# Last two batches of an early-fusion block: routing products in the score banks, batch 6 routed behind batch 7's rows, the last bias addition behind the scatter

## The reference

```python
h = tok_ref(x, ...)                       # ccm, curve, 3 channels -> 1, clipped
h = concatenate([h, txt], axis=1)         # 8 x 384 x 256
h = h + attn_ref(layernorm(h), W_DKV, W_UK, W_UV, W_UQ, W_O)
# ffn_ref(layernorm(h)):
scores = softmax(xf @ router_w)           # 3072 tokens x 8 experts
expert_weights, top_experts = top_k(scores, 2)
for k in range(2):                        # capacity 384 tokens per expert and k, in order of token
    y = dispatch_compute(xf, top_experts[:, k], w1, w2, capacity)
    out = out + y * expert_weights[:, k][:, None]
h = h + out + bias
```

## Time and profile before

| | us |
|---|---|
| three timed runs | 773.05, 773.74, 775.08 |
| their median | 773.74 |
| the profiled execution, device time | 771.72 |
| its span, from the first to the last instruction | 770.0 |
| first load of the expert half starts at | 467.35 |

### The profile page before, as it was taken

One profiled execution on the slowest core, in us unless ns is written; L12 is line 12 of the kernel. 1 busy time (PEld: TensorE's weight loads), 2 busy tenths in 40 slices (PEclk: granted clock), 3 DMA queues, 4 the chain that ended last, 5 costly groups with the idle time before them and its releaser, 6 DMA issues. The chain is left out here.

```text
span 770.0 us, 13676 instructions
## 1 busy us (share of the span) xinstructions
PE 644.2 (84%) x5136; PEld 517.6 (67%) x5136; DVE 419.1 (54%) x1003; ACT 388.3 (50%) x806; POOL 306.6 (40%) x393
## 2 busy tenths in 40 slices
PE   0435789998998999989998514999999999999993
PEld 0112445666665665656675314999999999999993
DVE  5522746868687886976875433544444444444320
ACT  2332547676574856746566004555445544554540
POOL 4100000010030402104042353977888888888234
PEclk9977989999999989999999655999999999999997
DMA  5155564637364442535620123444444444542113
GB/s 184 41 133 163 146 170 119 182 97 195 88 159 107 125 113 70 133 78 135 198 78 24 52 73 105 148 97 97 97 104 103 104 97 118 133 115 42 21 21 41
DMA packets 58978, 82.90 MB, mean 108 GB/s; under 512 B 6048, under 2 KB 50218, under 8 KB 58912
## 3 DMA queue, kind: packets, MB, share of 16 engines
q1 hardware_dynamic: 46480, 66.72, 30.3%
q0 software_dynamic: 9216, 12.41, 9.7%
q10 hardware_dynamic: 3216, 2.89, 1.2%
HBM read 50.30 MB, written 31.78 MB: 107 GB/s over the span
## 5 line engine op out<-in xcount | busy, mean ns | idle before, releaser
L1386 DVE TENSOR_TENSOR hl<-h,hh 128x384 fp32r<-128x384 f32 x128 | 103.6, 809 | 156.2 <-ACT h L1343 156.0
L921 DVE TENSOR_REDUCE mx<-s_bank 128x2 f32<-128x256 f32 (+2 forms) x192 | 124.3, 685 | 75.6 <-PE s_bank L505 74.9
L1340 ACT ACTIVATE hh<-t_bank 128x384 fp32r<-128x384 f32 x128 | 63.0, 492 | 133.5 <-PE t_bank L1428 131.2
L763 ACT ACTIVATE pt<-t_bank 128x512 f32<-128x512 f32 x128 | 76.4, 597 | 75.1 <-PE t_bank L526 73.2
L1309 POOL DMA_INDIRECT out<-yo,xr x48 | 74.8, 1558 | 72.2 <-ACT yo L1351 62.4
L1299 POOL TENSOR_TENSOR wl<-wr,wh 128x256 fp32r<-128x256 f32 x112 | 94.6, 877 | 1.2
L504 PE MATMUL s_bank<-ks,qs 96*128 96x128 bf16 (+2 forms) x384 | 81.5, 280 | 12.2 <-DMA ks<-qk_scratch 11.6
L525 PE MATMUL t_bank<-qs,ks 98*128 98x384 bf16 (+2 forms) x384 | 86.8, 278 | 5.0 <-DMA qs<-mT 4.2
L1428 PE MATMUL t_bank<-xh,wh 128*128 128x384 f32 x256 | 87.0, 340 | 0.0
L1428 PE MATMUL t_bank<-xl,wh 128*128 128x384 f32 x256 | 86.6, 338 | 0.0
L1428 PE MATMUL t_bank<-xh,wl 128*128 128x384 f32 x256 | 86.4, 337 | 0.0
(11 more groups left out here) (159 smaller groups left out, 1488.2 us busy)
## 6 DMA issues: line engine op xcount, KB each, us to landing
wr<-in_L_ffn_w SPq DMA_DIRECT2D x16, 1024.0 KB, 6.0
qk_scratch<-part SPq DMA_DIRECT2D x96, 96.0 KB
slot_rows<-empty SPq DMA_DIRECT2D x6, 1040.0 KB, 10.7
xr<-slot_rows SPq DMA_DIRECT2D x16, 390.0 KB, 3.3
wr<-in_x SPq DMA_DIRECT2D x7, 768.0 KB, 13.6
qs<-qk_scratch SPq DMA_DIRECT2D x16, 288.0 KB
ks<-qk_scratch SPq DMA_DIRECT2D x16, 288.0 KB
qs<-qk_scratch SPq DMA_DIRECT2D x16, 192.0 KB
```

The lines of the kernel that those rows point to most:

```text
L763: ins = act.activation(pt[:, p, unit // 2, 0:AT[1]], bank, ACT.Exp)
L921: ins = dve.tensor_reduce(mx[:, p // 2, j, 2 * (p % 2):2 * (p % 2) + 2], pair_region(s_bank, j), AX_X, ALU.max)
L1340: act.activation(hh[:, f, :], h_banks[f % NH], ACT.Gelu_apprx_tanh)
L1386: dve.tensor_tensor(hl[:, f, :], h[f % 2][:, :], hh[:, f, :].bitcast(F32), ALU.subtract).then_inc(hl_done, 1)
```

## The change

The batches 0 to 5 are untouched. For batches 6 and 7:

- The logits of the router go to `s_bank[0]` and the rank products to `s_bank[1]` instead of to `bank1`, with a ledger key of their own, "late".
- In turn 16 `contexts_back(15, 1)` stands before `router(6)`.
- `project(7, 1)` writes `s_bank[2]` and follows `project(7, 0)` in turn 16; DVE's two `residual(7)` follow each other there too.
- `ranks(6)` stands behind both. DVE's `keep_ranks(6)` stands behind `variances2(7)`, and `weigh(6)` and `place(6)` behind `scaled2(7)`.
- The second `rows_back(7)` writes `t_bank[2]` (M[1]) instead of `bank0`.
- POOL adds the bias of batch 7 behind its loop, that is behind `send(7)`; the store of batch 7 waits for it as before.

```diff
+        OVER = 2 * B
+        def logit_bank(b):
+            return C[:, T:T + NT * E] if b < B - 2 else s_bank[:, 0, 0:NT * E]
+        def rank_bank(b):
+            return C[:, T:T + NT * KE] if b < B - 2 else s_bank[:, 1, 0:NT * KE]
+        def project_bank(b, k):
+            return s_bank[:, 2, :] if b == B - 1 and k else M[0]
+        def rows_bank(b, c):
+            return M[1] if b == B - 1 and c else M[0]
...
@@ POOL
-                    if live(b - 1):
+                    if live(b - 1) and b < B:
                         residual(b - 1)
+            residual(B - 1)
             for q in range(2):
                 pool.wait_ge(sent[q], 16 * (B // 2) * NT * TOPK)
...
@@ TensorE, helpers
-            def project(b, k, bank):
+            def project(b, k):
                 pe.wait_ge(cn_sb, 2 * b + 2)
-                take(bank, hid_add, 2 * b + k + 1)
+                take("last" if b == B - 1 and k else 0, hid_add, 2 * b + k + 1)
+                dst = project_bank(b, k)
...
-            def rows_back(b, c, bank):
+            def rows_back(b, c):
                 pe.wait_ge(row_done, (NT + 1) * b + NT)
-                take(bank, rowT_sb, KC * b + c + 1)
+                take(1 if b == B - 1 and c else 0, rowT_sb, KC * b + c + 1)
...
+            def route_key(b):
+                return "C" if b < B - 2 else "late"
...
@@ TensorE, turns
                     if p == 1:
                         routed = not odd and live(b - 2)
-                        if routed:
+                        if routed and n < OVER:
                             router(b - 2)
                         if prev:
-                            contexts_back(n - 1, 1, routed)
+                            contexts_back(n - 1, 1, routed and n < OVER)
+                        if routed and n >= OVER:
+                            router(b - 2)
...
-                        routed = not odd and live(b - 2)
+                        routed = not odd and live(b - 2) and n != OVER
...
-                        if p == 0 and live(b - 1):
-                            project(b - 1, 1, 0)
+                        if p == 0 and live(b - 1) and n < OVER:
+                            project(b - 1, 1)
...
                         if p == 3 and live(b - 1):
-                            project(b - 1, 0, 0)
+                            project(b - 1, 0)
+                        if p == 3 and n == OVER:
+                            project(b - 1, 1)
+                            ranks(b - 2)
...
@@ DVE, turns
                     if odd:
-                        if p == 0 and live(b - 2):
+                        if p == 0 and live(b - 2) and n != OVER + 1:
                             weigh(b - 2)
                             place(b - 2)
-                        if p == 0 and live(b - 1):
-                            residual(b - 1, 1, 0)
+                        if p == 0 and live(b - 1) and n < OVER:
+                            residual(b - 1, 1)
                         if p == 1 and live(b - 1):
                             norms2(b - 1)
                             variances2(b - 1)
+                        if p == 1 and n == OVER + 1:
+                            keep_ranks(b - 2)
                         if p == 2 and live(b - 1):
                             scaled2(b - 1)
+                        if p == 2 and n == OVER + 1:
+                            weigh(b - 2)
+                            place(b - 2)
...
-                        if p == 3 and live(b - 2):
+                        if p == 3 and live(b - 2) and n != OVER:
                             keep_ranks(b - 2)
...
                         if p == 3 and live(b - 1):
-                            residual(b - 1, 0, 0)
+                            residual(b - 1, 0)
+                        if p == 3 and n == OVER:
+                            residual(b - 1, 1)
```

More of the change, by code:

```diff
@@ L578, in contexts_out @@
                 mm.then_inc(cnT_ps, 1)
-            def project(b, k, bank):
+            def project(b, k):
                 pe.wait_ge(cn_sb, 2 * b + 2)
-                take(bank, hid_add, 2 * b + k + 1)
+                take("last" if b == B - 1 and k else 0, hid_add, 2 * b + k + 1)
+                dst = project_bank(b, k)
                 for at, t in enumerate((0, 1) if k == 0 else (2,)):
                     for c in range(KC):
-                        mm = pe.matmul(M[bank][:, at * DIM:(at + 1) * DIM], cn[:, c, t * P:(t + 1) * P], wo[:, c, :],
+                        mm = pe.matmul(dst[:, at * DIM:(at + 1) * DIM], cn[:, c, t * P:(t + 1) * P], wo[:, c, :],
                                        start=(c == 0), stop=(c == KC - 1))
@@ L650, in ranks @@
                 pe.wait_ge(oh_done, b + 1)
-                take("C", step, ROUTER_STEPS * b + RANK_STEP)
+                take(route_key(b), step, ROUTER_STEPS * b + RANK_STEP)
                 for t in range(NT):
-                    dst = C[:, T + t * KE:T + (t + 1) * KE]
+                    dst = rank_bank(b)[:, t * KE:(t + 1) * KE]
                     pe.matmul(dst, tri[:, :], ohb[:, t, :], start=True, stop=False)
@@ L731, in _ @@
                         if p == 3 and live(b - 1):
[L732 removed]
+                            rows_back(b - 1, 1)
                     else:
@@ L828, in token_values, with rows_back @@
                 act.activation(vb[b % 2][:, tiles, :, 0:HD], src, ACT.Copy).then_inc(v_sb, 1)
-            def rows_back(b, c, bank):
+            def rows_back(b, c):
                 act.wait_ge(rowT_ps, KC * b + c + 1)
-                act.activation(rowT[:, c, :], M[bank][:, 0:T], ACT.Copy).then_inc(rowT_sb, 1)
+                act.activation(rowT[:, c, :], rows_bank(b, c)[:, 0:T], ACT.Copy).then_inc(rowT_sb, 1)
             def gates(b):
@@ L949, in normalise, with residual @@
                 dve.tensor_tensor(dst, src, by, ALU.mult).then_inc(cxn_done, 1)
-            def residual(b, k, bank):
+            def residual(b, k):
                 dve.wait_ge(wo_ps, 2 * b + k + 1)
                 tiles = slice(0, 2) if k == 0 else slice(2, 3)
-                src = M[bank][:, 0:(2 - k) * DIM].rearrange("p (t d) -> p t d", d=DIM)
+                src = project_bank(b, k)[:, 0:(2 - k) * DIM].rearrange("p (t d) -> p t d", d=DIM)
                 dve.tensor_tensor(hid[:, b, tiles, :], hid[:, b, tiles, :], src, ALU.add).then_inc(hid_add, 1)
@@ L1046, in choose @@
                 dve.wait_ge(log_ps, b + 1)
-                then(dve.tensor_copy(logits[:, :, :], C[:, T:T + NT * E].rearrange("p (t e) -> p t e", t=NT)))
+                then(dve.tensor_copy(logits[:, :, :], logit_bank(b).rearrange("p (t e) -> p t e", t=NT)))
                 for t in range(NT):
```

16 lines of the change are left out of this document (8 added, 8 removed).

## The result

| us | before | after |
|---|---|---|
| median of six timed runs each | 772.23 | 764.69 |
| their range | 768.05 to 775.08 | 763.59 to 767.08 |
| the profiled execution | 771.72 | 767.08 |
| last context copy to first load of the expert half | 43.79 | 37.85 |
| expert half, from that load to the end | 302.6 | 302.5 |

After divided by before is 0.9904, with a 95% interval from 0.9875 to 0.9934. The changed kernel is faster, by 0.66 to 1.25%. The forecast of 768.3 lies 3.6 above the measured time, and the lower end of its range 1.1.

A forecast was written before the change was run, and what follows sets the result against it. The bound was taken as the front half's tail, ending in POOL's last scatter and DRAIN. Terms of 5.78 us saved less 0.38 given back made 5.40, so 773.74 became 768.3 us; range 765.8 to 770.6.

The forecast's parts named there:

- The ranks: Batch 6's rank products moved behind the output product, which then starts 1.76 us sooner, 0.46 from the transposes included.
- The bank of the second part: Output product of batch 7: its second part no longer waits for DVE to empty the bank; 1.21 us saved.
- The stall of `shifted`: Batch 7's `shifted` takes 0.18 instead of 2.14 us once POOL's bias addition is gone from beside it; 1.96 saved.
- a POOL that becomes the bound by 2 us: Rival: all twelve scatter transfers stretch from 1.28 to 1.47 us; gain 3.3, time 770.4; chance 0.08.
- a late store: Rival: batch 7's store, issued last, lands at 469.5 and ends the front half; time 776.1; chance 0.03.
- a clock that stays down longer in the expert half: Rival: full clock returns later relative to the expert half's work; gain 2.7, time 771.0; chance 0.12.
- the context transposes before the router: Batch 6: three transposes go ahead of the router products, moving the logits copy and then cn 0.46 us sooner.
- rival 1: Full clock returns within the unbroken output products; 1.1 us more gain, time 767.2; chance 0.25.
- the tie that the forecast saw: Batch 6's scatter frees POOL at 448.13, only 0.2 us before batch 7's scatter wants it.
- The price of the addition: Bias addition behind POOL's last scatter delays the DRAIN at the barrier; 0.38 us given back.
- The weighed rule: Batch 6's transfers beside DVE's copies and casts for batch 7 lose up to 0.6 us in all; gain 4.8, not 5.4.
- the same 5.40 off it: Forecast time taken as the median of three timed runs, 773.74, less the front half's gain of 5.40: 768.3 us.

The follow-up runs named there:

- ranks_first: Changed kernel with the rank products of batch 6 ahead of the output product again; 767.04 us in a single run.
- bias_alone: Kernel before with only the last bias addition moved behind the last scatter; ratio 0.9943 to the kernel before.
- after_again: The changed kernel unedited, run once more on another chip; 811.52 us against 817.52 for the kernel before, ratio 0.9922.
- cn_first: Changed kernel with ScalarE copying cn ahead of the gates exponential of batch 6; 806.85 us against 816.55 for the kernel before, ratio 0.9863.
- warm_before: Kernel before with products nobody reads, 8 ahead of the ranks and 20 behind the output product's second part; ratio 0.9975.
- warm_experts: Changed kernel with unused products, 80 behind the ranks of batch 7 and 22 ahead of the expert half's first transposes; ratio 0.9871.
- rows_one_bank: Changed kernel with both row transposes of batch 7 in bank0; 769.4 us in a single run.
- bias_old: Changed kernel with the last bias addition put back before the last scatter; 812.97 us, ratio 0.992 to the kernel before.
- v2_cold: cn_first, with VectorE instead of POOL adding the biases of batches 6 and 7, behind batch 6's places; 810.87 us, ratio 0.9899.
- v2: v2_cold plus unused products: 3 ahead of the output product, 22 behind it, 80 behind batch 7's ranks, 22 before the expert transposes; ratio 0.9929.

## Why the prediction was right or wrong, point by point

The step that failed is the base that the gain was taken off, with a range that allowed for no spread of it (third step below). Two terms of the sum were off as well, in opposite directions (first and second step). Each term, and the same difference in the profiles of before and after:

| step | forecast | measured |
|---|---|---|
| last context copy to output product | -1.76 | 5.79 to 4.50, -1.29 |
| output product | -1.21 | 6.68 to 4.42, -2.26 |
| its end to the rows | 0 | 3.19 to 3.19, 0 |
| rows to logits | -0.85 | 6.91 to 6.00, -0.91 |
| logits to slots | -1.96 | 7.20 to 5.50, -1.70 |
| slots to the load | +0.38 | 14.02 to 14.24, +0.22 |
| sum | -5.40 | -5.94 |

**Right in mechanism and size.** The ranks cost 1.30 us of waiting (ranks_first 1.26). The bank of the second part is worth 1.21 at half clock, to the hundredth (6.68 before, 5.47 in ranks_first). The two banks of the transposes are worth 0.91 (undone, 0.90). The stall of `shifted` was the bias addition (1.95 of the 1.96 up to the slots in bias_alone; with its price at the barrier 1.74 alone, 1.86 undone). The DRAIN is a cost behind POOL's last work: it lasts 3.98 us when nothing runs ahead of it, and in after 4.22, because its record begins 0.21 before the addition ends; from that end it is 4.01. The store stayed hidden. The rivals of a POOL that becomes the bound by 2 us, of a late store, and of a clock that stays down longer in the expert half did not come: the expert half is 302.5 against 302.6.

**Wrong, first step: "the context transposes before the router", 0.46 sooner.** The logits did come sooner, by 0.64, and none of it reached the product. POOL adds the bias of batch 6 at 1.89 to 3.73 us behind the context copy before, at 1.92 to 3.76 after. `shifted` now comes at 2.99 and ends with the addition at 3.81, where the old one, begun at 3.62 with 0.11 of the addition still to run, took 0.18 and ended at 3.80. That the old one was not held was luck of its place. The addition of before:

```profile
425.45 1.84 POOL L439 TENSOR_TENSOR hid<-hid,bias 128x768 f32<-128x768 f32 x1
```

The exponential waits for `shifted` and cn stands behind it, so cn starts at 3.97 in both kernels. I had used this very collision as a term for batch 7, and did not ask what POOL does while batch 6's logits move. Where the addition was over earlier, on the chip of after_again, the product started at 3.99. cn_first takes the copy out of that chain altogether.

**Wrong, second step: the clock in the output product.** The sum took half clock throughout, rival 1 had the price (1.1) and the chance (0.25). It came, with 1.05. "Against: at half clock the old eight products brought nothing back" was a weak reason, since that was one execution; in warm_before the old product had the full clock for its second part. Over the nine profiles of the changed kernel and its variants without products of no use ahead of it the product takes 4.37 to 5.47 us. Three times it ran at half clock throughout or nearly so (ranks_first, after_again, warm_experts: 5.29 to 5.47), and in five it had about a microsecond of what full clock gives (after, rows_one_bank, bias_old, cn_first, v2_cold: 4.37 to 4.55). It should have been the likelier case.

**Smaller misses.** Logits to slots lost 0.19 of its gain in the cast of `slot_i` of batch 7: 0.36 us instead of 0.17, ending with POOL's last transfer of batch 6 at 448.57. So the tie that the forecast saw (0.2 us of margin) was a bound after all, here through the cast, and in v2 through POOL's queue. The price of the addition was 0.22 for 0.38. The weighed rule would have made the transfers beside DVE longer; they stayed at 0.97 to 1.04 us, and it was DVE that waited. The Trainium skill, "SBUF — State Buffer", section "Who interferes with whom", covers both stalls: a VectorE instruction with two inputs in SBUF contends with a GpSimd one that reads SBUF, and a cast in a two-port mode with any, and the one that comes second is blocked until the first ends. The 0.82 of `shifted` agrees, for it began inside the addition and ended with it. The 2.14 and the 2.42 end with the addition too, but their records begin 0.26 and 0.55 us before its own, so which came second they do not show, and the old `shifted` of batch 6, begun in the addition's last 0.11 us, was not visibly held. Whether the cast was held by the same lock no run here tests.

**Wrong, third step, and the one that decides: the base ("the same 5.40 off it") and the range.** These terms miss by 0.54 us, and 3.6 was missed. I took the forecast gain off the median of three runs, 773.74; six give 772.23, and that is 1.5. The three runs that came with the result have the median 769.83; 5.40 off that is 764.4, beside the 764.69 measured. Which of the runs of before were made together with those of the changed kernel is not on record, so this fit may be chance. Profile against profile the two kernels differ by 4.64 us in device time, although the tail gave 5.94, since the head of after happened to be 1.39 longer; the medians differ by 7.54. The interval of the ratio, 5.1 to 9.7 us, holds 5.94. The 1.6 between it and 7.54 has no place in any trace that I have, and the scatter of the head is large enough for it. That it is only scatter is likely but not shown. The range was built from the bounds of the terms alone. The spread of the base, 2 us in the three runs and 7 in the six, had no part in it; with it 764.69 would have lain inside.

## What to carry to other kernels

When an instruction moves, look at what the other engines run at its new time, not only at what it waited for at the old one: a gain of 0.64 us vanished in a collision that the same profile showed two rows further down. Where a result for the main chain stands in an engine's queue behind one for a side chain (cn behind the exponential), its order can be worth as much as the speed of either (0.64 us in cn_first). The same holds for a side chain that stands ahead of the main one on an engine: in warm_before a product faster by 0.95 brought 0.2. And a range for the time needs the spread of the base beside the bounds of the terms.

## What the runs showed of the hardware

- A small two-input operation on VectorE with both inputs in SBUF, 0.17 to 0.18 us alone, took 2.14 (before), 0.82 (after) and 2.42 us (bias_old) beside POOL's addition of 1.83 to 1.84 us, and ended within 0.1 us of it each time. One that began 0.11 us before the addition's end took 0.18.
- The cast of `slot_i` took 0.35 to 0.36 us instead of 0.17 in seven profiles, when it fell into the last part of a POOL indirect transfer, and ended with it. In rows_one_bank it came after that transfer and took 0.17. In after a cast of `top_i` at 444.26, inside the transfer of 443.74, took 0.16.
- Eight float32 products of the output product took 3.76 us at half clock. In the tail the full clock came and went by the execution: the same twelve products took 4.42 us in one profile and 5.29 in another of the same kernel, on another chip.
- POOL's DRAIN at the barrier lasted 3.98 us behind its last transfers (before, bias_old, v2_cold, v2), and ended 4.01 us after the addition where the addition came last (after).
- The tail of the kernel before repeated to 0.01 us in two profiles, while the attention half ahead of it varied by 5 us between executions of the same code.
